# Two wide one-hot tables of a sorting stage move from VectorE to ScalarE, and one of them becomes a table of signs

## The chip, the cores and the metric

The kernel runs on one core of one Trainium2 chip. The metric is the device time of one execution in microseconds (us); lower is better. The engines named below are TensorE (PE, with its weight loads PEld), VectorE (DVE), ScalarE (ACT), GpSimd (POOL) and the DMA queues, of which SyncE (SP) issues most.

## What is computed

A graph network of four layers over 6250 nodes with 128 features and 200000 edges. Each layer gathers the features of source nodes, sums them by destination node, multiplies by weights and ends in a residual and a layer norm. Cut to what matters:

```python
deg = jnp.maximum(segment_sum(ones, dst, 6250), 1.0)
x = _layernorm(x + _L0_gnn_ref(x, deg ** -0.5, W0, b0, src, dst))       # sum of (x W)[src] by dst
x = _layernorm(x + _L1_gnn_ref(x, w_neigh, w_self, b_self, src, dst))   # mean by dst
x = _layernorm(x + _L2_gnn_ref(x, edge_index, W1, b1, W2, b2))          # x + sum by dst, two layers
x = _layernorm(x + _L3_gnn_ref(x, edge_index, ...))                     # attention over edges, by src
```

The change touches none of this arithmetic on features. It lies in the preparation: the edges, which arrive ordered by destination, are also sorted by the 128-node tile of their source.

## The kernel before, in words

The program is a row of stages, each a block of its own with its own semaphores; every engine has to finish a stage before any starts the next. The first three sort the edges. `load_columns` loads source and destination indices and lays them out as 98 blocks (`BLOCKS`) of 128 x 16 edges. `rank_columns` gives each edge a place inside the list of its source tile. `permute_columns` sends each edge's record to that place in memory. Later stages build adjacency tiles, run the layers, and run the edge attention.

The change lies in `rank_columns` alone. Before it, the stage uses only VectorE and TensorE. VectorE and TensorE pass work to each other through semaphores, in the program order that is written out:

- At the start VectorE writes a few small constants (lines 265 to 267) and then `pick` (line 268), a table of 49 tiles x 128 columns that repeats each column of `tile_axis` 128 times. TensorE waits for it (`s_pick`, line 330) only before its first `ranks`.
- `hots(s)` (line 228) makes 49 one-hot rows of segment s, one for each tile. The 98 blocks are cut into four segments (`PARTS`, of 26, 24, 24 and 24 blocks). `counts` (line 313) sums the one-hots on TensorE as they appear.
- `offsets(s)` (lines 234 to 253) turns counts into running offsets in a chain of short VectorE steps, each waiting for the last. Line 251 copies `base`, the first row of each tile in each block; line 252 goes on from it.
- `select(s)` (line 263) takes 49 ranks from PSUM with predicated copies, each fed by two matmuls (lines 325 and 326, the second of which reads `pick`). The next segment's `hots` are issued before it.
- After the fourth segment come a few 49-row steps (lines 276 to 281), two small matmuls (lines 338 and 339), and then the large comparison of line 283: `own[t, b, r]` is 1 where row r of block b is at or past `base[t, b]`, and 0 elsewhere, over 98 x 128 = 12544 columns. It is written over `hot`, whose readers are done by then.
- VectorE then reads the matmuls' result (lines 285 and 286), forms `shift` (line 287), TensorE differences it (line 341), and VectorE splits it in two fp16 parts (`shift16`, lines 290 to 293). With that, TensorE contracts `own` with `shift16`, block by block (line 344, 98 matmuls of two columns each).
- Meanwhile VectorE turns the places into lane and row (lines 295 to 299), and then reads the 98 results into `dest` (lines 302 and 303), which ends the stage. The next stage's VectorE work begins at line 385, its ScalarE work at line 449 with the same kind of activation, `Sign` of a ramp plus a bias for each partition.

Of the kernel before, what the change touches and what calls it, by code (L numbers as in the profile page):

```python
# [4 lines left out]
F32 = mybir.dt.float32  # L5
F16 = mybir.dt.float16
# [3 lines left out]
ALU = mybir.AluOpType  # L10
ACT = mybir.ActivationFunctionType
AX = mybir.AxisListType

P = 128
# [3 lines left out]
NT = -(-N_NODES // P)  # L18
# [7 lines left out]
BLOCKS = -(-N_EDGES // (P * K))  # L26
# [157 lines left out]
def rank_columns(nc, m):  # L184


    PARTS = ((0, 26), (26, 50), (50, 74), (74, BLOCKS))
    SEGS = len(PARTS)
# [7 lines left out]
    with ExitStack() as ctx:  # L196
        sb = lambda n, s, d: ctx.enter_context(nc.sbuf_tensor(n, s, d))
        sem = lambda n: nc.alloc_semaphore("rk_" + n)
# [10 lines left out]
        first = sb("first_of_tile", [NT, 1], F32)  # L209
        shift, shifti, shift16 = sb("row_shift", [NT, BLOCKS], F32), sb("row_shift_int", [NT, BLOCKS], I32), sb("row_shift16", [NT, BLOCKS, 2], F16)  # L210
        lani = sb("place_int", [P, CC], I32)
        own = hot[0:NT, :, :, :].rearrange("t a n w -> t (a n w)")[:, 0:BLOCKS * P].rearrange("t (b r) -> t b r", r=P)
        ps = ctx.enter_context(nc.psum_tensor("rank_ps", [P, R, 512], F32))
        psc = ctx.enter_context(nc.psum_tensor("tile_count_ps", [P, 512], F32))
        psb = ctx.enter_context(nc.psum_tensor("row_base_ps", [P, 512], F32))
        psr = ctx.enter_context(nc.psum_tensor("row_ps", [P, 512], F32))
        s_hot, s_cnt, s_cnt_read, s_nrow, s_base, s_prefix, s_ranked, s_taken, s_chunks, s_first, s_shift, s_step, s_own, s_dest, s_pick, s_v = (
            sem(n) for n in ("hot", "cnt", "cnt_read", "nrow", "base", "prefix", "ranked", "taken", "chunks", "first", "shift", "step", "own", "dest", "pick", "v"))
        block = ctx.enter_context(nc.Block())

        @block.vector
        def _(dve):
            ch = Chain(dve, s_v)
            by_block = lambda t: t.rearrange("t (b k) -> t b k", k=K)

            def hots(s):
                for t in range(NT):
                    ins = nc.vector.tensor_scalar(hot[:, s % 2, t, 0:width(s)], m.tile16[:, cols(s)], float(t), None, ALU.is_equal)
                    if t % BITS == BITS - 1:
                        ins.then_inc(s_hot, 1)  # L230

            def offsets(s):

                blk, w, nb = slice(*PARTS[s]), width(s), PARTS[s][1] - PARTS[s][0]
                dve.wait_ge(s_cnt, s + 1)
                ch(nc.vector.tensor_tensor_scan(upto[:, 0:w], psc[0:T2, 0:w], m.lo_bias[0:T2, 0:w], carry[:, 0:1] if s else 0.0, ALU.add, ALU.bypass))
                ch(nc.vector.tensor_tensor(upon[:, 0:w], upto[:, 0:w], psc[0:T2, 0:w], ALU.subtract))
                dve.sem_inc(s_cnt_read, 1)
                nc.vector.tensor_copy(carry[:, :], upto[:, w - 1:w])
                ch(nc.vector.tensor_copy(upi[:, 0:w], upon[:, 0:w]))  # L240
                ch(nc.vector.tensor_scalar(ends[:, 0:nb], by_block(upto[:, 0:w])[:, :, K - 1], float(LANES - 1), None, ALU.add))
                ch(nc.vector.tensor_scalar(ends[:, 0:nb], ends[:, 0:nb], 6, None, ALU.arith_shift_right))
                ch(nc.vector.tensor_scalar(begs[:, 0:nb], by_block(upi[:, 0:w])[:, :, 0], 6, None, ALU.arith_shift_right))
                ch(nc.vector.tensor_tensor(nrow[:, blk], ends[:, 0:nb], begs[:, 0:nb], ALU.subtract))
                dve.sem_inc(s_nrow, 1)
                ch(nc.vector.tensor_scalar(low[:, 0:w], upi[:, 0:w], LANES - 1, None, ALU.bitwise_and))
                nc.vector.tensor_copy(prefix[0:64, 0:w], low[0:64, 0:w])
                nc.vector.tensor_copy(rowq[:, blk], begs[:, 0:nb])
                ch(nc.vector.tensor_tensor(upon[:, 0:w], upon[:, 0:w], low[:, 0:w], ALU.subtract))
                dve.wait_ge(s_base, s + 1)  # L250
                ch(nc.vector.tensor_copy(base[:, blk], psb[0:T2, 0:nb]))
                ch(nc.vector.tensor_tensor(adj[:, 0:nb], base[:, blk], rowq[:, blk], ALU.subtract))
                nc.vector.scalar_tensor_tensor(by_block(prefix[64:T2, 0:w]), adj[64:T2, 0:nb].unsqueeze(2).broadcast_to([NT, nb, K]), float(LANES),
                                               by_block(upon[64:T2, 0:w]), ALU.mult, ALU.add).then_inc(s_prefix, 1)

            def select(s):

                for t in range(NT):
                    i = s * NT + t
                    if i >= 2:  # L260
                        dve.wait_ge(s_taken, i - 1)
                    dve.wait_ge(s_ranked, i + 1)
                    nc.vector.copy_predicated(m.places[i % 2][:, cols(s)], hot[:, s % 2, t, 0:width(s)].bitcast(U16), ps[:, t % R, 0:width(s)]).then_inc(s_taken, 1)

            nc.vector.tensor_copy(before2[:, 0:64], m.before[0:NT, 0:64])
            nc.vector.tensor_copy(before2[:, 64:T2], m.before[0:NT, 0:NT])
            nc.vector.tensor_tensor(follow[:, :], m.ident[0:NT, 0:NT], m.shift1[0:NT, 0:NT], ALU.subtract)
            nc.vector.tensor_copy(pick[:, :, :], m.tile_axis[:, :].unsqueeze(2).broadcast_to([P, NT, P])).then_inc(s_pick, 1)
            hots(0)
            for s in range(SEGS):  # L270
                offsets(s)
                if s + 1 < SEGS:
                    hots(s + 1)
                select(s)

            ch(nc.vector.tensor_scalar(chf[:, :], carry[0:NT, :], float(2 * P - 1), None, ALU.add))
            ch(nc.vector.tensor_copy(chi[:, :], chf[:, :]))
            ch(nc.vector.tensor_scalar(chi[:, :], chi[:, :], 8, None, ALU.arith_shift_right))
            ch(nc.vector.tensor_copy(chf[:, :], chi[:, :]))
            ch(nc.vector.tensor_scalar(chf[:, :], chf[:, :], 1.0, 2.0, ALU.max, ALU.mult))  # L280
            nc.vector.tensor_scalar(chb[:, :], m.ones[0:NT, :], chf[:, 0:1], None, ALU.mult).then_inc(s_chunks, 1)

            ch(nc.vector.tensor_tensor(own, m.iota128h[0:NT, :].unsqueeze(1).broadcast_to([NT, BLOCKS, P]), base[0:NT, :].unsqueeze(2).broadcast_to([NT, BLOCKS, P]), ALU.is_ge))
            dve.wait_ge(s_first, 1)
            ch(nc.vector.tensor_scalar(first[:, :], psr[0:NT, 64:65], P / LANES, None, ALU.mult))
            nc.vector.tensor_copy(m.first_chunk[:, :], psr[:, 0:NT + 1])
            ch(nc.vector.scalar_tensor_tensor(shift[:, :], rowq[0:NT, :], first[:, 0:1], base[0:NT, :], ALU.add, ALU.subtract))
            dve.sem_inc(s_shift, 1)
            dve.wait_ge(s_step, 1)
            ch(nc.vector.tensor_copy(shifti[:, :], psr[0:NT, 256:256 + BLOCKS]))  # L290
            ch(nc.vector.tensor_scalar(shifti[:, :], shifti[:, :], LANES - 1, None, ALU.bitwise_and))
            nc.vector.tensor_copy(shift16[:, :, 0], shifti[:, :])
            nc.vector.tensor_tensor(shift16[:, :, 1], psr[0:NT, 256:256 + BLOCKS], shifti[:, :], ALU.subtract).then_inc(s_own, 1)
            dve.wait_ge(s_taken, SEGS * NT)
            ch(nc.vector.tensor_tensor(lani[:, :], m.places[0][:, 0:CC], m.places[1][:, 0:CC], ALU.min))
            ch(nc.vector.tensor_scalar(m.places[0][:, 0:CC].bitcast(I32), lani[:, :], LANES - 1, None, ALU.bitwise_and))
            ch(nc.vector.tensor_scalar(lani[:, :], lani[:, :], 6, None, ALU.arith_shift_right))
            nc.vector.tensor_copy(m.lane[:, 0:CC], m.places[0][:, 0:CC].bitcast(I32))
            nc.vector.tensor_copy(m.rowkey[:, 0:CC], lani[:, :])
            dve.wait_ge(s_dest, 1)  # L300
            dest2 = psb[:, 0:2 * BLOCKS].rearrange("p (b a) -> p b a", a=2)
            ch(nc.vector.tensor_scalar(m.dest[:, :], dest2[:, :, 0], m.row_id[:, 0:1], None, ALU.add))
            ch(nc.vector.tensor_tensor(m.dest[:, :], m.dest[:, :], dest2[:, :, 1], ALU.add))

        @block.tensor
        def _(pe):
# [33 lines left out]
            pe.wait_ge(s_shift, 1)  # L340
            nc.tensor.matmul(psr[0:NT, 256:256 + BLOCKS], follow[:, :], shift[:, :], start=True, stop=True).then_inc(s_step, 1)
            pe.wait_ge(s_own, 1)
            for b in range(BLOCKS):
                ins = nc.tensor.matmul(psb[:, 2 * b:2 * b + 2], own[:, b, :], shift16[:, b, :], start=True, stop=True)
            ins.then_inc(s_dest, 1)


# [1744 lines left out]
```

## Time and profile before

| | us |
|---|---|
| median of 3 runs | 4251.69 |
| lowest and highest run | 4246.45 and 4258.07 |
| the profiled execution, device time | 4245.02 |
| its span in the profile | 4243.3 |
| VectorE busy | 3012.9 (71%) |
| TensorE busy | 3502.5 (83%) |
| ScalarE busy | 2154.5 (51%) |

The profiled execution's own time is 1.7 us above its span. A page of the profile gives busy time by engine, the same in 40 slices of the span (106 us each, a digit for each tenth of busy share), and groups of instructions. Engine shares over the span mix stages with different limits; for a change in one stage the timeline of that stage is what is to be read, that is, instructions in order of their start, with the idle time before them in brackets and what ended it.

### The profile page before, as it was taken

To read this page: it belongs to the slowest core of one execution; us is meant where nothing else is said; L and a number is where in the kernel's file an instruction comes from. 1 tells how busy PE (TensorE), PEld (TensorE's weight loads), DVE (VectorE), ACT (ScalarE), POOL (GpSimd) and SP (SyncE) were. 2 spreads that over 40 slices of the span, in tenths; PEclk is the share of its full clock that TensorE was granted. 3 is DMA by queue.
4 is the path that set the end of the run, shared out by engine and by line. 5 is a ranking of instruction groups with operands and counts; after the bars stand their busy time and mean duration, and the time that the engine had idled before them with its cause. 6 is when DMAs were issued, how large, how long until landed. Compare 5 with 4: busy or idle time off the path is not lost. (4 is left out here: it accounts for less than half of the span.)

```text
span 4243.3 us, 93850 instructions
## 1 busy us (share of the span) xinstructions
PE 3502.5 (83%) x20539; PEld 2389.7 (56%) x20540; DVE 3012.9 (71%) x11949; ACT 2154.5 (51%) x6858; POOL 1538.0 (36%) x1256
## 2 busy tenths in 40 slices
PE   4868883698889899995998898688888888888884
PEld 2357782333333344443445344588888888888883
DVE  8999997798888888886002101688888888887785
ACT  0068895256677788885002101455555555555554
POOL 0058884100000000001002001277777777777770
PEclk8855555699999999997999999899999999999996
DMA  2011113001111222221884786355555555555551
GB/s 49 1 10 14 15 17 78 18 26 44 62 70 79 88 96 88 101 92 45 327 304 157 278 303 212 118 151 153 153 151 151 151 151 154 150 150 151 150 148 41
DMA packets 276486, 498.39 MB, mean 117 GB/s; under 512 B 92440, under 2 KB 192943, under 8 KB 276255
## 3 DMA queue, kind: packets, MB, share of 16 engines
q1 hardware_dynamic: 209922, 347.11, 24.4%
q0 software_dynamic: 66336, 149.10, 12.8%
q14 instruction: 191, 1.56, 0.1%
q8 instruction: 37, 0.61, 0.1%
HBM read 391.18 MB, written 104.89 MB: 117 GB/s over the span
## 5 line engine op out<-in xcount | busy, mean ns | idle before, releaser
L1694 POOL DMA_INDIRECT xs<-edge_table,ea_row_stage x1088 | 1085.1, 997 | 345.6 <-issue 329.3
L1245 PE MATMUL a_agg_ps<-a_adj_ring,parts 128*128 128x512 f16 (+1 forms) x2548 | 523.5, 369 | 47.1 <-DMA a_adj_ring<-adjacency 47.0
L1914 ACT ACTIVATE slot_dst<-ea_onehot,ea_mask 128x128 f32<-128x128 f16 x1632 | 535.8, 399 | 13.2
L1044 PE MATMUL ab_agg_ps<-ab_adj_stage,parts 128*128 128x512 f16 x1911 | 529.9, 388 | 0.0
L1868 PE MATMUL ea_psz<-parts,ea_onehot_t 128*128 x2176 | 307.7, 286 | 200.6 <-issue 182.5
L449 ACT ACTIVATE dst_step<-iota,dst_low_bias 128x128 f16<-128x128 f16 x1188 | 358.6, 405 | 216.0 <-PEq L474 213.0
L429 POOL DMA_INDIRECT records<-both_parts,record_row x98 | 350.4, 3576 | 309.9 <-ACT both_parts L455 285.6
L1908 ACT ACTIVATE ea_mask<-ea_dot,b 128x4 f32<-128x4 f32 x408 | 121.3, 297 | 671.0 <-DVE slot_src L1819 666.3
L1385 POOL TENSOR_TENSOR parts<-xs,parts 128x896 f16<-128x896 f32 x7 | 13.2, 1882 | 1226.7 <-ACT parts L1379 1226.7
L1879 PE MATMUL ea_psa<-xs,slot_dst 128*128 128x129 f32 x3264 | 437.5, 278 | 2.5 <-ACT slot_dst L1914 2.5
L1117 ACT ACTIVATE ab_src_off<-iota,ab_neg_src 128x128 f16<-128x128 f16 x712 | 282.2, 396 | 304.1 <-PE ab_adj_ps L1065 141.1
L1245 PEld LDWEIGHTS a_agg_ps<-a_adj_ring,parts 128*128 128x128 f16 x2548 | 242.1, 98 | 328.6 <-DMA a_adj_ring<-adjacency 48.0
L1879 PEld LDWEIGHTS ea_psa<-xs,slot_dst 128*128 128x128 f32 x3264 | 413.8, 194 | 9.8 <-DVE agg_t L1792 2.1
L1868 PEld LDWEIGHTS ea_psz<-parts,ea_onehot_t 128*128 128x128 f32 x2176 | 271.5, 196 | 225.6 <-issue 225.6
L1012 DVE TENSOR_SCALAR ab_dst_hot_middle<-iota,slot_dst 128x512 f16<-128x512 f16 x1218 | 395.0, 349 | 0.0
L1151 ACT ACTIVATE ab_adj_stage<-ab_adj_ps 128x512 f16<-128x512 f32 x637 | 371.9, 605 | 16.4 <-PE ab_adj_ps L1070 14.7
L1065 PE MATMUL ab_adj_ps<-ab_dst_hot_middle,ab_src_hot_middle 128*128 128x512 f16 x1218 | 337.8, 383 | 16.3 <-DVE ab_dst_hot_middle L1012 6.5
L1864 PE MATMUL ea_psv<-vx,xs 128*128 x1088 | 325.0, 380 | 0.0
L1862 PE MATMUL ea_psv<-vx,xs 128*128 x1088 | 324.3, 380 | 0.6 <-DVE xs L1781 0.6
L1044 PEld LDWEIGHTS ab_agg_ps<-ab_adj_stage,parts 128*128 128x128 bf16 x1911 | 190.3, 100 | 228.4 <-issue 19.1
L1792 DVE TENSOR_TENSOR agg_t<-agg_t,ea_psa 128x129 f32 x816 | 230.8, 283 | 96.7 <-PE ea_psa L1879 93.3
L1056 PE MATMUL ab_adj_ps<-ab_dst_hot_first,ab_src_hot_first 128*128 128x512 f16 x637 | 218.5, 391 | 84.7 <-DVE ab_dst_hot_first L1012 50.3
(387 smaller groups left out, 6433.5 us busy)
## 6 DMA issues: line engine op xcount, KB each, us to landing
a_adj_ring<-adjacency SPq DMA_DIRECT2D x182, 896.0 KB, 4.6
ea_low_rows<-low_rows SPq DMA_DIRECT2D x411, 128.0 KB
adjacency<-ab_adj_stage SPq DMA_DIRECT2D x91, 512.0 KB, 2.6
adjacency<-ab_adj_stage SPq DMA_DIRECT2D x91, 384.0 KB, 2.3
ea_near_rows<-near_rows SPq DMA_DIRECT2D x137, 128.0 KB
xs<-edge_table,ea_row_stage POOLq DMA_INDIRECT x1088
edge_table<-vx SPq DMA_DIRECT2D x12, 512.0 KB, 2.9
ea_row_stage<-row_columns SPq DMA_DIRECT2D x272, 2.0 KB
```

Of the source, the lines that this page charges most:

```text
L429: nc.gpsimd.indirect_dma_start(m.rec[q % 2], bass.IndirectOffsetOnAxis(ap=rows[:, q:q + 1], axis=0), both[:, q, :], None, compute_op=ALU.a ...
L449: ins = nc.scalar.activation(step[:, h, k, :], m.iota128h[:, :], ACT.Sign, bias=m.lo_bias[:, bass.ds(n * K + k, 1)])
L1012: return nc.vector.tensor_scalar(dst[:, k, :], m.iota512[:, :], float(t * SPAN), m.slot_dst[:, bass.ds(c, 1)], ALU.add, ALU.is_equal)
L1044: ins = nc.tensor.matmul(agg_ps[:, :], lhs(r, t), stage[:, k, :], start=start and r == 0, stop=stop and r == parts - 1)
L1065: nc.tensor.matmul(ps[:, k, :], src_m[:, k, :], dst_m[:, k, :], start=False, stop=False).then_inc(s_used_m[k], 1)
L1151: nc.scalar.activation(stage[:, k, :], ps[:, k, :], ACT.Copy, accum_out=col(m.out_deg, n * TG + k)).then_inc(s_taken[k], 1)
L1245: ins = nc.tensor.matmul(ps[:, h, 0:width], lhs(r, t), ring[:, g % SLOTS, k * DB:k * DB + width], start=t == 0 and r == 0, stop=t == NT - ...
L1694: nc.gpsimd.indirect_dma_start(got[:, h, g, k, 0:ROW], None, m.table, bass.IndirectOffsetOnAxis(ap=row_s[:, h, g, k:k + 1], axis=0)).then_ ...
L1864: ins = nc.tensor.matmul(psv[:, k, :, :].rearrange("p c d -> p (c d)"), hot_d[:, 1, k, :], pair(1), start=False, stop=True)
L1868: ins = nc.tensor.matmul(psz[:, g, k, :], hot_t[:, g, k, :], of(m.u, tile_at(tiles[k])), start=True, stop=True)
L1879: ins = nc.tensor.matmul(psa[:, g, k // 2, 0:AW], hot_m[:, g, k, :], what, start=k % 2 == 0, stop=k % 2 == 1)
L1914: ins = nc.scalar.activation(hot_m[:, g, k, :], hot[:, h, g, :, k], ACT.Copy, scale=mask[:, g, k:k + 1])
```

## The change

ScalarE gets a part of its own in the stage. It writes `pick` at its beginning. Then, as each segment's `base` is known (a new semaphore `s_under`, counted up by a new VectorE step after line 251), it makes for each block of the segment a 49 x 128 tile of signs in a new buffer `side`, out of the same ramp, with `0.5 - base` as bias. The sign is +1 where `own` had 1, and -1 where it had 0. The comparison of line 283 is gone. A sign table stands for `2 own - 1`, so TensorE adds a second matmul for each block, with a table of ones (`always`) in the same PSUM columns, and the two closing steps multiply by one half. The wait for `s_side` stands in TensorE's queue before that loop.

```diff
+        always = sb("always", [NT, P], F16)
+        side, under = sb("row_side", [NT, BLOCKS, P], F16), sb("row_under", [NT, BLOCKS], F32)
...
+        @block.scalar
+        def _(act):
+            nc.scalar.activation(pick[:, :, :], m.tile_axis[:, :].unsqueeze(2).broadcast_to([P, NT, P]), ACT.Copy).then_inc(s_pick, 1)
+            for s in range(SEGS):
+                act.wait_ge(s_under, s + 1)
+                for b in range(*PARTS[s]):
+                    ins = nc.scalar.activation(side[:, b, :], m.iota128h[0:NT, :], ACT.Sign, bias=under[:, b:b + 1])
+            ins.then_inc(s_side, 1)
...
                 ch(nc.vector.tensor_copy(base[:, blk], psb[0:T2, 0:nb]))
+                nc.vector.tensor_scalar(under[:, blk], base[0:NT, blk], -1.0, 0.5, ALU.mult, ALU.add).then_inc(s_under, 1)
...
+            nc.vector.memset(always[:, :], 1.0)
...
-            nc.vector.tensor_copy(pick[:, :, :], m.tile_axis[:, :].unsqueeze(2).broadcast_to([P, NT, P])).then_inc(s_pick, 1)
...
-            ch(nc.vector.tensor_tensor(own, m.iota128h[0:NT, :].unsqueeze(1).broadcast_to([NT, BLOCKS, P]), base[0:NT, :].unsqueeze(2).broadcast_to([NT, BLOCKS, P]), ALU.is_ge))
...
-            ch(nc.vector.tensor_scalar(m.dest[:, :], dest2[:, :, 0], m.row_id[:, 0:1], None, ALU.add))
-            ch(nc.vector.tensor_tensor(m.dest[:, :], m.dest[:, :], dest2[:, :, 1], ALU.add))
+            ch(nc.vector.tensor_scalar(m.dest[:, :], dest2[:, :, 0], 0.5, m.row_id[:, 0:1], ALU.mult, ALU.add))
+            ch(nc.vector.scalar_tensor_tensor(m.dest[:, :], dest2[:, :, 1], 0.5, m.dest[:, :], ALU.mult, ALU.add))
...
             pe.wait_ge(s_own, 1)
+            pe.wait_ge(s_side, 1)
             for b in range(BLOCKS):
-                ins = nc.tensor.matmul(psb[:, 2 * b:2 * b + 2], own[:, b, :], shift16[:, b, :], start=True, stop=True)
+                nc.tensor.matmul(psb[:, 2 * b:2 * b + 2], side[:, b, :], shift16[:, b, :], start=True, stop=False)
+                ins = nc.tensor.matmul(psb[:, 2 * b:2 * b + 2], always[0:NT, :], shift16[:, b, :], start=False, stop=True)
             ins.then_inc(s_dest, 1)
```

## Rows read from the trace of the kernel before

**Rows 1.** The page: span, busy time by engine, and ScalarE in 40 slices.

```profile
span 4243.3 us, 93850 instructions
PE 3502.5 (83%) x20539; PEld 2389.7 (56%) x20540; DVE 3012.9 (71%) x11949; ACT 2154.5 (51%) x6858; POOL 1538.0 (36%) x1256
ACT  0068895256677788885002101455555555555554
```

**Rows 2.** Timeline, start of the stage: start, length (us), engine, line, operation, count, [idle].

```profile
40.93 0.20 DVE L267 TENSOR_TENSOR less_previous<-ident,shift_one 49x49 f32<-49x49 f32 x1
41.05 6.67 DVE L268 COPY tile_pick<-tile_axis 128x6272 f16<-128x6272 f16 x1
47.64 8.74 DVE L228 TENSOR_SCALAR tile_hot<-src_tile 128x416 f16<-128x416 f16 x49
...
77.03 0.10 PEld L325 LDWEIGHTS rank_ps<-tile_hot,before 128*128 128x128 f16 x1
```

**Rows 3.** Timeline, end of the stage.

```profile
214.25 13.21 DVE L283 TENSOR_TENSOR tile_hot<-iota,row_base 49x12544 f16<-49x12544 f16 x1
...
214.97 0.32 PE L339 MATMUL row_ps<-chunks,before 49*49 49x1 f32 x2
227.50 0.15 DVE L285 TENSOR_SCALAR first_of_tile<-row_ps 49x1 f32<-49x1 f32 x1
...
229.64 1.77 DVE L295 TENSOR_TENSOR place_int<-slot_src,slot_dst 128x1568 int32<-128x1568 f32 x1
...
229.78 2.77 PE L344 MATMUL row_base_ps<-row_shift,tile_hot 49*128 49x2 f16 x98 [1.00 <-DVE row_shift L293]
...
235.25 0.32 DVE L302 TENSOR_SCALAR block_rows<-row_base_ps,row_id 128x98 f32<-128x98 f32 x1
235.60 0.26 DVE L303 TENSOR_TENSOR block_rows<-block_rows,row_base_ps 128x98 f32<-128x98 f32 x1
```

**Rows 4.** Timeline, `offsets` of the fourth segment.

```profile
186.26 0.16 DVE L248 CAST chunk_of_tile<-row_begins 113x24 f32<-113x24 int32 x1
186.34 0.54 DVE L249 TENSOR_TENSOR count_before<-count_before,count_low 113x384 f32<-113x384 f32 x1
186.92 0.18 DVE L251 COPY row_base<-row_base_ps 113x24 f32<-113x24 f32 x1
187.14 0.18 DVE L252 TENSOR_TENSOR row_adjust<-row_base,chunk_of_tile 113x24 f32<-113x24 f32 x1
```

**Rows 5.** Timeline of ScalarE alone, from the last stage to the next.

```profile
20.44 3.06 ACT L137 ACTIVATE dst_rows<-dst_cols_ps 128x1664 int32<-128x1664 f32 x1 [4.70 <-PE dst_cols_ps L129]
236.53 7.12 ACT L449 ACTIVATE dst_step<-iota,dst_low_bias 128x128 f16<-128x128 f16 x24 [213.03 <-PEq L474]
```

**Rows 6.** Groups of ScalarE by line: count, busy us, mean ns of one, idle before.

```profile
L449 ACT ACTIVATE dst_step<-iota,dst_low_bias 128x128 f16<-128x128 f16 x1188 | 358.6, 405 | 216.0 <-PEq L474 213.0 <-PE degree_ps L495 2.0 <-issue 1.0
L455 ACT ACTIVATE both_parts<-perm_ps 128x128 f32<-128x128 f32 x98 | 26.8, 273 | 0.0
L624 ACT ACTIVATE parts<-scaled 128x896 bf16<-128x896 f32 x14 | 13.2, 944 | 22.2 <-POOL scaled L600 22.2
```

**Rows 7.** Single lines 344 and 339: duration in ns (min/median/max), first and last start.

```profile
L344 PE MATMUL row_base_ps<-row_shift,tile_hot x98: 162/162/182, 229.8 to 232.4; 49*128 49x2 f16 x98
L339 PE MATMUL row_ps<-chunks,before x2: 218/229/240, 215.0 to 215.1; 49*49 49x1 f32 x2
```

**Rows 8.** Stretches: length, then busy us (count) by engine, TensorE's granted clock, DMA.

```profile
109.00:110.00 1.00, 0.71 (x3) 0.54 (x4) 1.00 (x7) 0.00 (x0) 0.00 (x0) 0.50 0.00 0
112.00:113.00 1.00, 1.00 (x8) 0.81 (x7) 1.00 (x8) 0.00 (x0) 0.00 (x0) 0.99 0.00 0
188.00:189.00 1.00, 1.00 (x4) 0.49 (x5) 0.10 (x1) 0.00 (x0) 0.00 (x0) 0.50 0.00 0
193.00:194.00 1.00, 1.00 (x5) 0.46 (x4) 0.91 (x2) 0.00 (x0) 0.00 (x0) 0.53 0.00 0
212.00:237.00 25.00, 4.48 (x106) 3.79 (x106) 23.29 (x29) 0.47 (x2) 0.00 (x0) 0.55 0.00 0
```

More of the change, by code:

```diff
@@ L211, in rank_columns @@
         lani = sb("place_int", [P, CC], I32)
-        own = hot[0:NT, :, :, :].rearrange("t a n w -> t (a n w)")[:, 0:BLOCKS * P].rearrange("t (b r) -> t b r", r=P)
+        always = sb("always", [NT, P], F16)
+        side, under = sb("row_side", [NT, BLOCKS, P], F16), sb("row_under", [NT, BLOCKS], F32)
         ps = ctx.enter_context(nc.psum_tensor("rank_ps", [P, R, 512], F32))
@@ L216, in rank_columns @@
         psr = ctx.enter_context(nc.psum_tensor("row_ps", [P, 512], F32))
-        s_hot, s_cnt, s_cnt_read, s_nrow, s_base, s_prefix, s_ranked, s_taken, s_chunks, s_first, s_shift, s_step, s_own, s_dest, s_pick, s_v = (
-            sem(n) for n in ("hot", "cnt", "cnt_read", "nrow", "base", "prefix", "ranked", "taken", "chunks", "first", "shift", "step", "own", "dest", "pick", "v"))
+        s_hot, s_cnt, s_cnt_read, s_nrow, s_base, s_prefix, s_ranked, s_taken, s_chunks, s_first, s_shift, s_step, s_own, s_dest, s_pick, s_under, s_side, s_v = (
+            sem(n) for n in ("hot", "cnt", "cnt_read", "nrow", "base", "prefix", "ranked", "taken", "chunks", "first", "shift", "step", "own", "dest", "pick", "under", "side", "v"))
         block = ctx.enter_context(nc.Block())
+        @block.scalar
[6 more added lines that the diff above has]
+            ins.then_inc(s_side, 1)
         @block.vector
```

## The prediction

> **What bounds the kernel now.** I read the page first, then the timeline of the stage. On the page [rows 1] TensorE is busy 83% of the span and VectorE 71%, and ScalarE 51%; but those are means over stages. The 40 slices of ScalarE begin with 0 0 6: it does almost nothing while the edges are ranked. The timeline says the same in one row: between its copy at line 137, which starts at 20.44, and its first `Sign` at 236.53 it sits idle for 213.03 us [rows 5]. So in `rank_columns` the engine that gets the work has nothing else to do, and the question is only what VectorE's two wide operations hold up.
>
> Both are on the path. At the start, `pick` takes VectorE from 41.05 to 47.64, and the one-hots of the first segment begin behind it; TensorE has nothing to count until they come [rows 2]. At the end, the comparison of line 283 starts at 214.25 and the next step of VectorE at 227.50, though the two small matmuls whose result that step reads were done at 214.97 + 0.32 = 215.29 [rows 3]. In the whole stretch from 212 to 237 TensorE is busy 4.48 us of 25 and VectorE 23.29 [rows 8]. VectorE is what sets the time there. As each stage ends before the next begins, time taken off this chain moves everything behind it forward.
>
> **What goes.** The comparison: line 285 started at 227.50 and can now start when line 339's result is there, at 215.29, plus some 0.05 for the hand-over. That is 12.2 us, not the 13.2 of the operation, since 1 us of it lay beside the matmuls. `pick` on VectorE: 47.64 - 41.05 = 6.6 us from start to start. Together 18.8 us.
>
> **What comes on VectorE.** One memset of 49 x 128 fp16. The trace shows no such row; the small step before `pick` takes 0.12 from its start to the next start (40.93 to 41.05) [rows 2]; I take 0.1, between 0.08 and 0.3. Four steps that make `0.5 - base` (49 x 24 or 26). None is waited for by the next instruction, so each costs a start-to-start distance: 0.08 where a step of that size is not waited for (line 248 to 249), 0.22 where it is (251 to 252) [rows 4]. They stand in the chain of `offsets`, which nothing covers. I take 0.1 each, since it is of the first kind: 0.4 in all, between 0.3 and 0.9. The closing steps at lines 302 and 303 (0.32 and 0.26 [rows 3]) get one more factor on 98 columns; I take 0.05 together, between 0 and 0.1.
>
> **What comes on ScalarE.** `pick` is 6272 columns. Two of its groups give a slope: 896 columns take 944 ns and 128 take 273, so 0.874 ns a column, and 6272 take 0.27 + 6144 x 0.000874 = 5.6 us [rows 6]; the worst row is line 137's strided copy, 3.06 us for 1664 columns or 1.84 ns each, which would be 11.5 us [rows 5]. Begun at 41, it is done between 46.7 and 52.5. TensorE first needs it at 77.03 [rows 2], now some 6.5 us earlier, at 70.5. Hidden by 18 us or more. The 98 signs are the same activation as line 449's: 24 in 7.12 us, 0.297 each when queued one behind another [rows 5], and by the mean of a single one, 405 ns, no worse than 0.41 each [rows 6]. That is 7.1 to 10.5 us for a segment, and 29 to 40 us in all, in an engine that stood idle for 213. The last segment's `base` is there at about 187.1 before, 180.4 after, so the table is complete by 190.2 at the latest. TensorE's loop that reads it began at 229.78 [rows 3] and will begin near 211. Its new wait, on `s_side`, has 20 us of slack; behind it in the queue stands only that loop, and VectorE's line 302 waits for the loop. Should this cover go, each us would count in full. Nothing else waits on ScalarE in the stage, and its queue is free again long before line 449.
>
> It is worth asking whether a simple copy belongs on ScalarE. VectorE's `pick` took 6.67 us for 6272 columns, 1.06 ns each [rows 2], slower than the 0.874 worked out for ScalarE. The Trainium skill (ScalarE: Activation LUTs, Rules for kernel authors) advises VectorE for simple elementwise work, up to three times as fast in 16-bit. By that rule `pick` on VectorE would be about a third of ScalarE's 5.6, some 1.9 us, and taking it away would give 4.7 us less than I count, a gain of 13.5. This repeated column does not run so; the row decides.
>
> **What comes on TensorE.** The loop of line 344 goes from 98 to 196 matmuls of two columns. The 98 took 2.77 us with 0.162 for the last one's own length, so (2.77 - 0.162) / 97 = 0.0269 us from start to start [rows 3, 7], at the lower level of the clock, 1.2 GHz (0.55 of full speed granted on average in the stretch [rows 8]). At this pace 196 take 5.43 us, from 229.78 to 235.21 in old times. VectorE, in lines 295 to 299, reaches line 302 at 235.25 [rows 3]. So the added 2.64 us are just covered and cost 0, with nothing to spare. The unknown is whether the second matmul of a pair, which adds to PSUM columns just written, keeps this pace. Below the row it cannot gain anything, as VectorE is then the later one. The upper bound is line 339: an fp32 product of one column runs as two instructions into one column, 0.32 us together at 0.218 for the shortest, so the second starts within 0.10 of the first [rows 3, 7]. With 0.10 for each second one the loop takes 98 x 0.127 + 0.16 = 12.6 us and is 7.1 us late. I take 0: the same line with the same shapes is nearer than an fp32 one, whose weights take longer to load.
>
> A rule bears on this. The Trainium skill (TensorE: Matmul & The Clock Gate, Back-to-back issue gap) gives a floor of about 25 ns for small matmuls, or about 62 ns each where instructions are decoded in software. By the latter the loop would take 12.3 us, be 6.9 late, and the gain would be 11.3. The trace's 27 ns agrees with the former.
>
> **The sum.** 12.2 + 6.6 - 0.1 - 0.4 - 0.05 = 18.2 us (rounded). The profiled execution took 4245.02, so 4226.8 for one like it. It lies 6.7 under the median of the three runs, 4251.69, and the prediction is for the median: 4251.69 - 18.2 = 4233.5.
>
> **Rivals.** (1) The pairs run slower than 27 ns. For it: no row shows two fp16 matmuls of two columns into the same place. Against it: line 339's second pass did not wait out the 218 ns of the first. At the bound 18.2 - 7.1 = 11.1 us, 4240.6.
>
> (2) TensorE's clock gives part back. After a pause the granted clock stays at 0.5 for a time that differs from segment to segment: in the second, restarted near 109.3, it is at 0.99 by 112; in the fourth, restarted at 188.0, it is still at 0.53 in 193 to 194 [rows 8]. That is 2.7 against 5.9 us. All the work shifts, so each of four segments may get another of these. A stretch at half the clock costs at most half its length, so 1.6 us a segment and 6.4 in all, up or down. All down: 11.8 us, 4239.9.
>
> (3) TensorE issues all 196 at some longer fixed pace, not only the second of each pair. At the mean of the row's 0.027 and line 339's 0.10, 0.0635 each, the loop takes 12.6 us and the time is rival 1's, 4240.6. Against it: the 98 of today would have taken 6.2 us so, and took 2.77. Software decoding, in the page named above, would be such a pace.
>
> (4) Slower than before: in the loop every matmul waits for its predecessor's result to be in PSUM, because of the open sum in the same bank. The price is line 344's whole length, 0.162 [rows 7], times 196, 31.8 us, or 26.3 beyond VectorE's arrival: 4251.69 - 18.2 + 26.3 = 4259.8. It decides from (18.2 + 5.5) / 196 = 0.12 us a matmul on, 4.5 times the pace of the row. Line 339 speaks against it again.
>
> (5) The change does not bring what it says: the sign table is late after all, or a later stage takes back what this one gives. The first needs 1.3 us a sign, over four times 0.297. The second needs a transfer whose time is set from outside the stage, and I see none that runs across it. 4251.7.
>
> **How the numbers follow.** Forecast 0.74; rival 1 0.10; rival 2 0.08; rival 3 0.02; rival 4 0.02; rival 5 0.04. About 0.3% of the time, 12.8 us, is what a measurement can tell from no change; faster than that means under 4238.9. The forecast's own range, by its bounds and part of rival 2, is 4229 to 4238, and the three runs before differ by 11.6 us among themselves, so some of it is lost: faster 0.70 of the forecast's 0.74, and 0.06 of rivals 1 to 3 in their milder forms, 0.76. Slower 0.03, from rivals 4 and 5. Within 0.3%: 0.21. The range goes down to 4224, for a gain of 21 with a fast set of runs (half of the runs' spread), and up to 4246, over rivals 1 to 3 with 5 us of spread.
>
> **What would show it.** In the timeline after: the one-hots of line 228 start near 41.2; ScalarE's `pick` beside them in 5 to 6 us; no idle time of TensorE before its first rank that ends on ScalarE; signs in four groups of 7 to 8 us; line 285 within 1.3 us of line 281's start; the loop of 196 matmuls in 5.4 us, and line 302 with at most 0.2 us of idle time; the next stage beginning near 218 instead of 236.4. The prediction is wrong if line 302 waits for TensorE by several us, if the segments' lengths between `offsets` change by more than 2 us each, or if the stage is 18 us shorter and the whole is not.

## The result

The changed kernel took 4233.81 us (median of 7 runs, 4226.92 to 4241.26) against 4254.39 (7 runs, 4243.41 to 4259.51) before. The ratio is 0.9957, with a 95% interval of 0.9943 to 0.9971: 18.3 us less on 4254.39, between 12 and 24 (the two medians as they stand lie 20.6 apart). Forecast were 18.2 us less and 4233.5.

| | before | after |
|---|---|---|
| median, us | 4254.39 | 4233.81 |
| profiled execution, us | 4245.02 | 4232.93 |
| its span | 4243.3 | 4231.2 |
| VectorE busy | 3012.9 | 2994.9 |
| ScalarE busy | 2154.5 | 2188.8 |

The page of the changed kernel, in the lines that answer to [rows 1]:

```profile
span 4231.2 us, 94148 instructions
PE 3503.2 (83%) x20637; PEld 2391.9 (57%) x20638; DVE 2994.9 (71%) x11952; ACT 2188.8 (52%) x6957; POOL 1547.7 (37%) x1256
ACT  2178884266677788884002001455555555555544
```

VectorE lost 18.0 us of busy time and ScalarE gained 34.3. ScalarE's first two slices went from 0 0 to 2 1. The start of the stage in the timeline (start, length, engine, line, operation, count, idle before), against [rows 2]:

```profile
40.72 5.43 ACT L224 ACTIVATE tile_pick<-tile_axis 128x6272 f16<-128x6272 f16 x1 [18.08 <-PEq L77]
40.78 0.17 DVE L276 MEMSET always<- 49x128 f16 x1 [0.60 <-PEq L77]
40.88 0.12 DVE L277 COPY before_twice<-before 49x64 f32<-49x64 f32 x1
...
41.13 8.76 DVE L238 TENSOR_SCALAR tile_hot<-src_tile 128x416 f16<-128x416 f16 x49
```

The one-hots start at 41.13, not 47.64, while ScalarE writes the table of tiles beside them. The chain of `offsets` in the fourth segment, against [rows 4]:

```profile
181.49 0.18 DVE L261 COPY row_base<-row_base_ps 113x24 f32<-113x24 f32 x1
181.71 0.17 DVE L262 TENSOR_SCALAR row_under<-row_base 49x24 f32<-49x24 f32 x1
181.79 0.17 DVE L263 TENSOR_TENSOR row_adjust<-row_base,chunk_of_tile 113x24 f32<-113x24 f32 x1
```

The added step (line 262) costs the distance to the next start, 0.08 us. The end of the stage, against [rows 3]:

```profile
208.71 0.28 DVE L292 TENSOR_SCALAR chunks_wide<-ones,chunks 49x128 f32<-49x128 f32 x1
209.50 0.32 PE L349 MATMUL row_ps<-chunks,before 49*49 49x1 f32 x2
209.85 0.15 DVE L295 TENSOR_SCALAR first_of_tile<-row_ps 49x1 f32<-49x1 f32 x1 [0.86 <-PE row_ps L349]
212.00 1.78 DVE L305 TENSOR_TENSOR place_int<-slot_src,slot_dst 128x1568 int32<-128x1568 f32 x1
217.36 0.16 PE L356 MATMUL row_base_ps<-row_shift,always 49*128 49x2 f16 x1
217.61 0.32 DVE L312 TENSOR_SCALAR block_rows<-row_base_ps,row_id 128x98 f32<-128x98 f32 x1
218.75 6.32 DVE L397 TENSOR_SCALAR dst_tile_hot<-dst_tile 128x224 f16<-128x224 f16 x49 [0.54 <-PEq L196]
```

VectorE now waits 0.86 us for the small matmul where it used to work through the comparison. The last of the 196 matmuls ends at 217.52, and line 312 starts at 217.61 with no idle time before it: covered, by 0.1 us. The next stage's VectorE work starts at 218.75 and started at 236.41 before. ScalarE's timeline, against [rows 5]:

```profile
57.84 7.70 ACT L228 ACTIVATE row_side<-iota,row_under 49x128 f16<-49x128 f16 x26 [11.69 <-DVE row_under L262]
100.91 7.13 ACT L228 ACTIVATE row_side<-iota,row_under 49x128 f16<-49x128 f16 x24 [35.37 <-DVE row_under L262]
...
181.91 7.12 ACT L228 ACTIVATE row_side<-iota,row_under 49x128 f16<-49x128 f16 x24 [33.54 <-DVE row_under L262]
218.88 7.12 ACT L461 ACTIVATE dst_step<-iota,dst_low_bias 128x128 f16<-128x128 f16 x24 [29.86 <-PEq L486]
```

Each group of signs is over in 7 to 8 us, and after the last, done at 189.0, ScalarE is idle for 29.86 us until the next stage.

### The profile page after: what moved, and what is told of

Same layout as the page of the kernel before. It is cut to its first block and busy times, and to the rows that moved or that the text cites. A ratio compares the mean times of both kernels' runs of the same rounds, so it can differ in the third digit from the quotient of the medians.

```text
span 4231.2 us, 94148 instructions
## 1 busy us (share of the span) xinstructions
PE 3503.2 (83%) x20637; PEld 2391.9 (57%) x20638; DVE 2994.9 (71%) x11952; ACT 2188.8 (52%) x6957; POOL 1547.7 (37%) x1256
## 5 line engine op out<-in xcount | busy, mean ns | idle before, releaser
L1077 PE MATMUL ab_adj_ps<-ab_dst_hot_middle,ab_src_hot_middle 128*128 128x512 f16 x1218 | 338.0, 384 | 15.8 <-DVE ab_dst_hot_middle L1024 6.9
```

The lines of the kernel that those rows point to most:

```text
L1077: nc.tensor.matmul(ps[:, k, :], src_m[:, k, :], dst_m[:, k, :], start=False, stop=False).then_inc(s_used_m[k], 1)
```

## The experiments

The theory to be tested: VectorE's chain sets the time of this stage, both wide operations lay on it, ScalarE and the longer matmul loop are covered, and the stages behind pass the gain on. The rivals are that the gain comes from one end only, that ScalarE's work is not free, that TensorE's loop is what ends the stage, or that later stages take part of it back. Each kernel was compared with the kernel before on its own chip. `e1_pick_only`, `e2_signs_only`, `e4_signs_late` and `e6_vector_pieces` ran on one where the kernel before takes 4671.93 us, all others where it takes 4249.3 or so; starts of stages are read against `before_again`, since no profile of the kernel before was taken on the other chip.

### The yardstick: both kernels once more on one chip

`before_again` is the kernel before and `after_again` the changed kernel, with no edit.

> The kernel before itself, unchanged, as the yardstick of this set: ratio 1.000, and its next stage begins near 236.4. It tells how far the ratios of two sets of executions of one program lie apart, and gives a profile from this chip beside the others.

> The changed kernel itself in the same set: ratio 0.9957, 18 us less, and the next stage begins near 218.7. If the first part gives 6.5 and the two together 18, the second gives 11.5, as it did alone (0.9974).

Measured: ratios 1.0004 (0.9995 to 1.0014) and 0.9955 (0.9939 to 0.9971). Their VectorE rows at the end of the stage and the start of the next, first `before_again`:

```profile
214.22 0.28 DVE L281 TENSOR_SCALAR chunks_wide<-ones,chunks 49x128 f32<-49x128 f32 x1
227.67 0.15 DVE L285 TENSOR_SCALAR first_of_tile<-row_ps 49x1 f32<-49x1 f32 x1
236.58 6.32 DVE L385 TENSOR_SCALAR dst_tile_hot<-dst_tile 128x224 f16<-128x224 f16 x49 [0.55 <-PEq L196]
```

and `after_again`:

```profile
208.06 0.28 DVE L292 TENSOR_SCALAR chunks_wide<-ones,chunks 49x128 f32<-49x128 f32 x1
209.35 0.15 DVE L295 TENSOR_SCALAR first_of_tile<-row_ps 49x1 f32<-49x1 f32 x1 [1.01 <-PE row_ps L349]
218.25 6.32 DVE L397 TENSOR_SCALAR dst_tile_hot<-dst_tile 128x224 f16<-128x224 f16 x49 [0.54 <-PEq L196]
```

Up to `chunks_wide` 214.22 - 208.06 = 6.16 us were gained, from there to `first_of_tile` 13.45 - 1.29 = 12.16, and in all 236.58 - 218.25 = 18.33. On 4249.27 that is a ratio of 0.9957, inside the interval: the stage alone is enough to account for the whole.

### One part at a time

`e1_pick_only` and `e1_again` are one kernel: the kernel before, with only the table of tiles moved.

```diff
-            nc.vector.tensor_copy(pick[:, :, :], m.tile_axis[:, :].unsqueeze(2).broadcast_to([P, NT, P])).then_inc(s_pick, 1)
+        @block.scalar
+        def _(act):
+            nc.scalar.activation(pick[:, :, :], m.tile_axis[:, :].unsqueeze(2).broadcast_to([P, NT, P]), ACT.Copy).then_inc(s_pick, 1)
```

> The kernel before with one part of the change: ScalarE writes the table of tiles, the large comparison stays on VectorE. My theory (VectorE's chain sets the time of the stage, so each part gives what it held up from start to start): the one-hots start 6.6 us earlier, ratio to before 0.9985, 6.5 us less. Rival (later TensorE work or its clock takes the start's gain back, and all of the 18 us comes from the end of the stage): no change, 1.000, with the fourth segment's last rank at the same time as before.

> The table of tiles on ScalarE alone, once more. The first look gave 0.9976 (0.9967 to 0.9985) where its timeline has the next stage only 5.5 us earlier, 0.9987. My theory (the stage passes on what it gains and no more): 0.9985, 6 us. Rival (this part saves more behind the stage than in it): 0.9976 or less again, 10 us.

Measured: 0.9976 (0.9967 to 0.9985) and then 0.9985 (0.9977 to 0.9994). Neither interval reaches 1.000, so the rival that nothing would change falls. The second is the 6.5 us of the theory (0.15% of 4249 is 6.4), and both timelines say less than 6.5. In `e1_again`:

```profile
208.57 0.28 DVE L284 TENSOR_SCALAR chunks_wide<-ones,chunks 49x128 f32<-49x128 f32 x1
222.02 0.15 DVE L288 TENSOR_SCALAR first_of_tile<-row_ps 49x1 f32<-49x1 f32 x1
230.93 6.32 DVE L388 TENSOR_SCALAR dst_tile_hot<-dst_tile 128x224 f16<-128x224 f16 x49 [0.55 <-PEq L196]
```

The comparison still takes its 13.45 us, and the next stage begins 5.65 us earlier than in `before_again`. The first set's 0.9976 was not borne out on this chip: a saving of 10 us lies just outside the second interval. The two intervals overlap, so this speaks against the rival that this part saves more behind the stage, but does not settle it for the first chip.

`e2_signs_only` is the changed kernel with the table of tiles back on VectorE.

```diff
-            nc.scalar.activation(pick[:, :, :], m.tile_axis[:, :].unsqueeze(2).broadcast_to([P, NT, P]), ACT.Copy).then_inc(s_pick, 1)
...
+            nc.vector.tensor_copy(pick[:, :, :], m.tile_axis[:, :].unsqueeze(2).broadcast_to([P, NT, P])).then_inc(s_pick, 1)
             hots(0)
```

> The kernel before with the other part: VectorE keeps the table of tiles, the table of rows comes as signs from ScalarE and the comparison goes. My theory: 12.2 us less at the end and 0.45 us more in the chains of offsets, 11.7 less in all, ratio 0.9972. From line 281's start to line 302's start 8.9 us instead of 21.2. Rival (all from the end): 18 us less, 0.9957.

Measured: 0.9974 (0.9963 to 0.9985), where 0.9972 was expected of the theory and 0.9957 of the rival, which lies outside. Its next stage begins at 225.15 in its profile, 11.4 us before 236.58. So the parts add, as far as whole runs can tell: 0.9985 x 0.9974 = 0.9959, and with the first set's 0.9976, from the same chip as 0.9974, 0.9950, against 0.9955 and 0.9957 for both together. By the start of the next stage they give 5.65 + 11.43 = 17.1 us, against 18.33; the rest is of the size of the differences in TensorE's clock that are told below.

### ScalarE's cover, used up and overdrawn

`e4_signs_late` waits for the fourth segment before the first sign. `e5_signs_late_twice` does the same and makes the 98 signs twice, the first time into a part of `hot` whose readers are done.

```diff
-            for s in range(SEGS):
-                act.wait_ge(s_under, s + 1)
-                for b in range(*PARTS[s]):
+            act.wait_ge(s_under, SEGS)
+            for b in range(BLOCKS):
                     ins = nc.scalar.activation(side[:, b, :], m.iota128h[0:NT, :], ACT.Sign, bias=under[:, b:b + 1])
```

> The changed kernel, but ScalarE waits for the fourth segment's base before it makes any sign, so that all 98 come in one run of 98 x 0.297 = 29.1 us, from 181.9 to 211.0. TensorE's loop reads them from 212.1 on. My theory: the slack of 20 us was real and this uses all but 1 us of it; the time is that of the changed kernel, ratio to before 0.9957. Rival (ScalarE's activations run at 0.405 each beside the ranks, or their writes slow VectorE's predicated copies): 98 x 0.405 = 39.7 us, ready at 221.6 and 9.5 us late, ratio 0.998.

> The changed kernel with ScalarE waiting for the fourth base and then making the 98 signs twice, the first time into memory that nobody reads: 196 x 0.297 = 58.2 us from 181.9, ready at 240.1 instead of 189. My theory (ScalarE's cover is one of place, not of kind; once past TensorE's loop at 212.1, each us counts in full): TensorE waits 28 us for ScalarE, and the loop is then uncovered too, so line 312 starts at 240.1 + 5.4 = 245.5, 28 us later than in the changed kernel: slower than before by 10 us, ratio 1.0023. Rival (the next stages absorb part of it): under 20 us later, ratio under 1.000.

Measured: 0.9952 (0.9938 to 0.9965) and 1.002 (1.001 to 1.003). ScalarE in `e4_signs_late`:

```profile
181.59 28.73 ACT L227 ACTIVATE row_side<-iota,row_under 49x128 f16<-49x128 f16 x98 [135.44 <-DVE row_under L261]
218.71 7.12 ACT L460 ACTIVATE dst_step<-iota,dst_low_bias 128x128 f16<-128x128 f16 x24 [8.39 <-PEq L485]
```

98 signs in 28.73 us, 0.293 each, while TensorE and VectorE ranked the last segment beside them. They are over at 210.32, TensorE's loop begins at 211.97, and nothing is late: the rival's 0.405 each falls. In `e5_signs_late_twice` the waits (who waited for whom, us in total, times, longest) are:

```profile
PE row_base_ps L356 <- ACT row_side L229: 28.1, 1, 28.1
DVE block_rows L313 <- PE row_base_ps L357: 26.9, 1, 26.9
```

Now TensorE waits for ScalarE, and VectorE for TensorE. Its next stage begins at 245.21 in its profile, 26.96 us later than in `after_again` and 8.6 later than in `before_again`; 1.002 of 4249.32 is 8.5. The forecast was 28 and 10. Nothing behind the stage took any of it up.

### TensorE's loop, doubled and halved

`e3_loop_twice` does each pair of the last loop twice. `e7_one_wide` does one matmul of 196 columns by the table of ones ahead of 98 of two columns.

```diff
-                nc.tensor.matmul(psb[:, 2 * b:2 * b + 2], side[:, b, :], shift16[:, b, :], start=True, stop=False)
-                ins = nc.tensor.matmul(psb[:, 2 * b:2 * b + 2], always[0:NT, :], shift16[:, b, :], start=False, stop=True)
+                for again in (0, 1):
+                    nc.tensor.matmul(psb[:, 2 * b:2 * b + 2], side[:, b, :], shift16[:, b, :], start=True, stop=False)
+                    ins = nc.tensor.matmul(psb[:, 2 * b:2 * b + 2], always[0:NT, :], shift16[:, b, :], start=False, stop=True)
```

```diff
             pe.wait_ge(s_side, 1)
+            nc.tensor.matmul(psb[:, 0:2 * BLOCKS], always[0:NT, :], shift16[:, :, :].rearrange("t b a -> t (b a)"), start=True, stop=False)
             for b in range(BLOCKS):
-                nc.tensor.matmul(psb[:, 2 * b:2 * b + 2], side[:, b, :], shift16[:, b, :], start=True, stop=False)
-                ins = nc.tensor.matmul(psb[:, 2 * b:2 * b + 2], always[0:NT, :], shift16[:, b, :], start=False, stop=True)
+                ins = nc.tensor.matmul(psb[:, 2 * b:2 * b + 2], side[:, b, :], shift16[:, b, :], start=False, stop=b == BLOCKS - 1)
```

> The changed kernel with each pair of TensorE's last loop done twice, 392 matmuls instead of 196, the same result. My theory (the loop was just covered by VectorE's lines 305 to 309, with nothing to spare): the loop takes 392 x 0.0269 + 0.16 = 10.7 us, line 312 waits for it and starts 5.2 us later, ratio to before 0.9970 instead of 0.9957. Rival (the loop has slack of its own, or is paced by something other than its count): less than 2 us, the ratio of the changed kernel.

> The changed kernel with one matmul of 196 columns by the table of ones ahead of the loop, instead of 98 of two columns inside it: 99 matmuls in some 3.0 us instead of 5.4. My theory: VectorE reaches line 312 no sooner, so nothing changes, ratio to before 0.9957. Rival (TensorE's loop is what line 312 waits for in the changed kernel): up to 2.4 us less, ratio 0.9951.

Measured: 0.9966 (0.9952 to 0.9979) and 0.9957 (0.9943 to 0.997). VectorE in `e3_loop_twice`:

```profile
216.84 0.97 DVE L309 CAST row_in_block<-place_int 128x1568 f16<-128x1568 int32 x1
222.91 0.32 DVE L312 TENSOR_SCALAR block_rows<-row_base_ps,row_id 128x98 f32<-128x98 f32 x1 [5.10 <-PE row_base_ps L357]
```

The wait appears at once. From line 305 (212.11) to line 312 it is 10.80 us instead of 5.61, 5.19 more where 5.2 was worked out beforehand. The ratio alone would not have shown it, as its interval also covers the changed kernel's 0.9957. TensorE in `e7_one_wide`:

```profile
212.53 0.34 PE L354 MATMUL row_base_ps<-row_shift,always 49*128 49x196 f16 x1 [1.01 <-DVE row_shift L303]
212.67 2.79 PE L356 MATMUL row_base_ps<-row_shift,row_side 49*128 49x2 f16 x98
```

The loop is over at 215.46 and line 312 starts at 217.99 with no wait, 5.61 us after line 305 at 212.38, as in the changed kernel (212.00 to 217.61). The ratio's interval covers theory and rival; the timeline decides for the theory. The loop was covered, and it sits right at the edge of its cover.

`e8_tail` goes on from there: ScalarE also takes one of VectorE's two last casts.

```diff
+            act.wait_ge(s_places, 1)
+            nc.scalar.activation(m.lane[:, 0:CC], m.places[0][:, 0:CC].bitcast(I32), ACT.Copy)
...
-            nc.vector.tensor_copy(m.lane[:, 0:CC], m.places[0][:, 0:CC].bitcast(I32))
```

> As the one with one wide matmul, and ScalarE takes one of VectorE's two casts behind the loop (the lanes) as well. Now both sides of the tail are shorter. My theory: one cast less on VectorE, 0.9 us from start to start, line 312 starts 0.9 us earlier than in the changed kernel, ratio to before 0.9955; too small for the ratio to tell, so the timeline is to show it. Rival (ScalarE's cast of 1568 columns, some 1.5 us, ends the stage later than VectorE does): no earlier start of the next stage.

Measured: 0.9952 (0.9938 to 0.9965); its interval covers that of the changed kernel. In the timeline line 307 (the old 305) starts at 212.08 and line 314 (the old 312) at 216.92, which is 4.84 instead of 5.61 us: 0.77 less, where 0.9 was expected (the new semaphore step puts 0.11 us between lines 308 and 310). The next stage begins at 218.06, 5.98 us after line 307 instead of 6.75. ScalarE's cast of 1.51 us began at 214.96, so it ended before VectorE did. The rival falls, and the step is too small for whole runs to show.

### Without ScalarE

`e6_vector_pieces` and `e6_again` are one kernel: VectorE makes both tables in pieces of 128 columns.

```diff
-            nc.vector.tensor_copy(pick[:, :, :], m.tile_axis[:, :].unsqueeze(2).broadcast_to([P, NT, P])).then_inc(s_pick, 1)
+            nc.vector.memset(ones16[:, :], 1.0)
+            ch(nc.vector.tensor_copy(axis32[:, :], m.tile_axis[:, :]))
+            for t in range(NT):
+                ins = nc.vector.tensor_scalar(pick[:, t, :], ones16[:, :], axis32[:, t:t + 1], None, ALU.mult)
+            ins.then_inc(s_pick, 1)
...
-            ch(nc.vector.tensor_tensor(own, m.iota128h[0:NT, :].unsqueeze(1).broadcast_to([NT, BLOCKS, P]), base[0:NT, :].unsqueeze(2).broadcast_to([NT, BLOCKS, P]), ALU.is_ge))
+            for b in range(BLOCKS):
+                nc.vector.tensor_scalar(own[:, b, :], m.iota128h[0:NT, :], base[0:NT, b:b + 1], None, ALU.is_ge)
```

> The kernel before without ScalarE: VectorE makes both tables itself, in 49 and 98 pieces of 128 columns with a scalar for each partition instead of one wide operation with a repeated operand. The one-hots of 224 and 384 columns take 0.129 and 0.171 us each in such a form, so 128 columns are estimated at 0.104. Theory (the wide operations ran at 1.05 ns a column because of the repeated operand, and VectorE's faster form gets part of the gain without another engine): 49 x 0.104 = 5.1 for the tiles and 98 x 0.104 = 10.2 for the rows, 4.4 us less in all, ratio 0.9990. Rival (pieces cost more than they save, at the 0.2 us of the small steps in the chain): 9.8 and 19.6, 9 us more, ratio 1.002.

> VectorE alone in 49 and 98 pieces, once more. In the first look its pieces took 0.164 us each instead of 0.104 and its next stage began 5.5 us later than before's, yet the ratio was 0.9999 (0.9987 to 1.0011). My theory (as above): 1.0013, 5.5 us more. Rival (what the stage loses comes back behind it): 1.000.

Measured: 0.9999 (0.9987 to 1.0011) and 1.0031 (1.0019 to 1.0044). The pieces in `e6_vector_pieces`:

```profile
41.35 8.05 DVE L272 TENSOR_SCALAR tile_pick<-ones,tile_axis 128x128 f16<-128x128 f16 x49
217.11 16.00 DVE L289 TENSOR_SCALAR tile_hot<-iota,row_base 49x128 f16<-49x128 f16 x98
```

8.05 / 49 = 0.164 and 16.00 / 98 = 0.163 us a piece, where 0.104 was estimated from one-hots that compare with a constant. The first theory's 4.4 us less falls, and so does the rival's 0.2 a piece. 8.05 replaces 6.67 and 16.00 replaces 13.21, and in `e6_again` the next stage begins at 241.58, 5.0 us later than in `before_again`. The whole runs agree neither with that, 1.0012, nor with each other: one set lies below it and the other above, and the two intervals do not meet. In `e6_again` the next stage (the permutation) took 443.0 us instead of 439.5, which makes 8.5 us in all, 1.0020, at the edge of its interval; this is taken up below under later stages. On the first chip the sorting stage was no different (`chunks_wide` of `e1_pick_only` at 208.61, of `e1_again` at 208.57), but the matmuls of the edge attention spread over 1844.7 us in `e1_pick_only` and 1826.5 in `e6_vector_pieces`, against 1415.3 in `e1_again`. Two profiles there differ by 18 us in that stage alone, so its ratios say little of effects of 5 us. What can be said is that VectorE alone did not gain.

## Why the prediction was right

**The comparison.** Forecast 12.2 us, since 1 us of it lay beside the small matmuls. Measured between `chunks_wide` and `first_of_tile`: 13.45 against 1.14 us (12.3), and 12.16 in the second pair. The 0.86 to 1.01 us of idle time at line 295 is the part that was rightly not counted. The closing steps cost nothing instead of 0.05.

**The table of tiles.** Forecast 6.6 less 0.1. The one-hots start 47.64 - 41.13 = 6.51 us earlier, and the four added steps take back 4 x 0.08 = 0.32 where 0.4 was forecast. That would leave 6.2 us at `chunks_wide`. It was 5.34 in the first pair of profiles and 6.16 in the second, and 5.65 in `e1_again`, which has no added steps. The difference is rival 2's mechanism. TensorE restarts at half its clock after each pause, and the full clock comes back sooner or later. In the second segment's counting, before (length, busy of PE, PEld, DVE, ACT, POOL, clock, DMA),

```profile
67.00:68.00 1.00, 0.57 (x2) 0.48 (x3) 1.00 (x7) 0.00 (x0) 0.00 (x0) 0.50 0.00 0
71.00:72.00 1.00, 1.00 (x8) 0.81 (x7) 1.00 (x7) 0.00 (x0) 0.00 (x0) 0.97 0.00 0
```

and after

```profile
59.00:60.00 1.00, 0.03 (x1) 0.06 (x2) 1.00 (x7) 1.00 (x5) 0.00 (x0) 0.50 0.00 0
65.00:66.00 1.00, 1.00 (x5) 0.67 (x5) 1.00 (x8) 0.54 (x2) 0.00 (x0) 0.56 0.00 0
```

that is 3.6 us at half the clock before and 5.9 after. Worked out in the same way from rows of 1 us, the stretches from TensorE's restart to the full clock are, in us:

| | counting, segments 1 to 4 | sum | ranks of segment 4 |
|---|---|---|---|
| `before` | 5.0, 3.6, 2.7, 4.0 | 15.3 | 6.0 |
| `after` | 2.9, 5.9, 3.8, 4.5 | 17.1 | 6.2 |
| `before_again` | 3.0, 6.0, 4.0, 4.6 | 17.6 | 2.9 |
| `after_again` | 5.4, 3.8, 2.7, 3.9 | 15.8 | 5.9 |
| `e1_again` | 4.2, 3.2, 5.9, 5.6 | 18.9 | 3.4 |

What such a us costs can be read too. From the first count of segment 2 to VectorE's first rank it is 10.32 us in `before` and 11.49 in `before_again`, so 2.4 us more at half the clock cost 1.2, one half. The ranks of segment 4 took 24.36 and 23.49 us, so 3.1 us cost 0.87, 0.28 each; there TensorE's two matmuls for a copy set a pace of 0.64 us at half the clock, and VectorE's copies one of 0.48 at the full one. An estimate for the gain at `chunks_wide` from these prices is 6.51 - 0.32 - 0.9 - 0.06 = 5.2 in the first pair, 6.47 - 0.32 + 0.9 - 0.84 = 6.2 in the second and 6.56 - 0.65 - 0.14 = 5.8 for `e1_again`: what was measured, to 0.2. So the clock did move in every segment, by up to 3 us, and it was luck that the sum stayed under 1 us of the 6.4 that rival 2 allowed for. Why the clock comes back when it does, no run told. The segments' lengths from one `base` to the next changed by 1.2 us at most, inside the 2 that the prediction had set as a sign of being wrong.

**ScalarE.** `pick` was put at 5.6 us and took 5.43, over at 46.15, and TensorE's first rank came at 70.69; signs at 0.297 took 7.12 / 24 = 0.297. The rule of the Trainium skill (ScalarE: Activation LUTs, Rules for kernel authors) that was weighed, simple work on VectorE, up to three times as fast, did not hold for the table of tiles: with a repeated operand VectorE took 6.67 us, in pieces 8.05, and ScalarE 5.43. For the table of rows VectorE was the faster engine, 13.21 us against 98 x 0.297 = 29.1 on ScalarE. That move paid only because ScalarE stood idle, and the comparison was on the path.

**TensorE.** 196 matmuls were put at 5.43 us; they ran from 212.14 to 217.52, 5.38 us. The second matmul of a pair, into columns just written, keeps the pace of 0.027. So rivals 1, 3 and 4 (0.10 for each second one, 0.0635 on average, or 0.162 each) fall together. In the sum this term was 0, and the two runs that changed the loop show why: it is 0 only up to 0.1 us.

**Later stages.** The first pair of profiles differs by 4245.02 - 4232.93 = 12.1 us and not 18, which taken alone would have read as rival 5. In the second pair the executions took 4245.71 and 4228.58, 17.1 less. Marks behind the stage tell where the first pair's 6 us went. The permutation, from the next stage's first one-hots to this row, first of the kernel before and then of the changed one,

```profile
676.11 0.47 DVE L639 RECIPROCAL inv_deg<-deg 128x49 f32<-128x49 f32 x1
```

```profile
662.92 0.47 DVE L651 RECIPROCAL inv_deg<-deg 128x49 f32<-128x49 f32 x1
```

took 676.11 - 236.41 = 439.7 us before and 662.92 - 218.75 = 444.2 after. In the second pair it is 439.5 and 443.6. The matmuls of the edge attention (count, ns, first and last start), first before and then after,

```profile
L1879 PE MATMUL ea_psa<-xs,slot_dst x3264: 272/275/578, 2739.8 to 4155.6; 128*128 128x129 f32 x192
```

```profile
L1891 PE MATMUL ea_psa<-xs,slot_dst x3264: 273/275/578, 2720.4 to 4143.6; 128*128 128x129 f32 x192
```

spread over 1415.8 and 1423.2 us. In the second pair that is 1416.0 and 1419.5. What lies between the two marks is shorter after, 2063.7 against 2057.5 us in the first pair and 2064.3 against 2057.9 in the second. So behind the stage the changed kernel lost 4.5, gained 6.2 and lost 7.4 us in the first pair, 5.7 lost in all, and in the second it lost 4.1, gained 6.4 and lost 3.5, 1.2 in all. The first two differences are the same in both pairs and look like properties of the two programs; the third is not. The medians of many executions show no sum of them beyond their intervals. The permutation's length does not follow the change itself: the profiles of the kernel before, of `e4_signs_late` and of `e7_one_wide` have 439 us, all the others 442.5 to 444. In it ScalarE waits 48.8 us for the records' transfers in `after_again` and 45.1 in `before_again`. Why is open; no run told it apart. The prediction had no term for it, and for what lies between the marks neither: that the two nearly cancel is luck.

**What was luck, and a slip.** The median came within 0.3 us of the 4233.5 forecast, but that figure was counted from a median of three, 4251.69, where seven executions gave 4254.39; the gain, 18.2 against 18.3 with an interval of 12 to 24 and 17.7 and 18.3 by the stage's own rows, is what bears the forecast out. And in rival 5 the 1.3 us a sign is where the sign table begins to be late; to lose the whole gain a sign would have to take about (30.6 + 18.2) / 24 = 2.0.

## What to carry to other kernels

An engine that is idle for a whole stage can take a table even if it needs longer for it in busy time (34.3 us against 18.0 here); what counts is when its first reader comes, and the timeline gives that to 0.1 us before anything is built. Count a removed operation from start to start of its neighbours, less what lay beside it. And judge a gain of 18 us in 4250 by the stage's own rows and by medians: one pair of profiles said 12, though the stage had given 17.7. Even the stage's own rows move by 1 us with TensorE's clock.

## What was not expected of the hardware

A VectorE comparison of 128 fp16 columns with a scalar for each partition takes 0.163 us from start to start (the product that made the tiles 0.164), while 224 columns compared with a constant take 6.32 / 49 = 0.129. The one form costs some 0.06 us more an instruction than the estimate from the other, 0.104, so cutting a wide operation into many such pieces lost here.
